# Window attention and a 3x3 convolution in one kernel: in every second window the two heads of a pair change halves of the key axis

## Time and profile before

| | |
|---|---|
| median of 3 runs | 3809.45 us (3807.93 to 3814.52) |
| profiled execution: span from the first to the last instruction | 3811.0 us |
| profiled execution: time of its own beside the span | none is recorded; its span stands 0.04% over the median of the runs |
| busy: TensorE matmul, weight load | 92%, 75% of the span |
| busy: VectorE, ScalarE, GpSimd | 81%, 69%, 61% |
| mean granted TensorE clock | 0.97 of 2.4 GHz |
| DMA | 10.5% of 16 engines, 27 GB/s of HBM traffic |

### The profile page before, as it was taken

How to read it: one execution, slowest core, us unless ns; L and a number is a source line. 1 busy time by engine, 2 the same in 40 slices (tenths; PEclk the granted TensorE clock), 3 DMA queues, 4 the chain that set the end, 5 groups by cost and what they waited for, 6 DMA issues and landing times.

```text
span 3811.0 us, 154831 instructions
## 1 busy us (share of the span) xinstructions
PE 3499.2 (92%) x57227; PEld 2843.6 (75%) x57227; DVE 3074.2 (81%) x7552; ACT 2642.8 (69%) x5857; POOL 2316.9 (61%) x3674
## 2 busy tenths in 40 slices
PE   2999999999999999999999999999999999999997
PEld 1677777777777777777777777777777777777775
DVE  5788877888878888788888788887788887888885
ACT  1877776777766677767777667767767777677773
POOL 4476555666555665556765556655556655566663
PEclk9999999999999999999999999999999999999998
DMA  2011110111101111101111101111011111111001
GB/s 54 19 32 34 32 30 24 31 32 34 32 25 27 34 34 32 32 22 32 32 34 34 27 25 32 34 33 33 22 29 32 34 34 27 27 30 34 17 17 30
DMA packets 213494, 115.45 MB, mean 30 GB/s; under 512 B 8784, under 2 KB 212688, under 8 KB 212688
## 3 DMA queue, kind: packets, MB, share of 16 engines
q1 hardware_dynamic: 212688, 104.72, 10.5%
HBM read 53.31 MB, written 51.38 MB: 27 GB/s over the span
## 4 chain that ended last, share of the span: by engine, by line
POOL 48%; issue 38%; PE 7%; DVE 3%; POOLq 2%; ACT 1%; SPq 0%; DMA 0%; DVEq 0%; ACTq 0%
POOL s_sb L408 21%; POOL plane L436 11%; POOL x_n L448 7%; POOL x_n L425 4%; PE conv_ps L998 2%; PE qkv_ps L879 2%; POOL gn_t L392 1%; POOL gn_t L394 1%; PE attn_ps L917 1%; POOL gn_t L393 1%; POOL gn_y L395 1%; PE probsT_ps L903 1%; PE scores_ps L892 1%; POOLq L388 1%; POOLq L405 1%
## 5 line engine op out<-in xcount | busy, mean ns | idle before, releaser
L408 POOL TENSOR_TENSOR s_sb<-s_sb,s_max 113x392 f32<-113x392 f32 x1024 | 1028.1, 1004 | 1304.8 <-DVE s_max L752 1304.4
L464 ACT ACTIVATE probs<-s_sb 113x392 f32<-113x392 f32 x1024 | 551.7, 539 | 195.6 <-POOL s_sb L408 136.9
L903 PE MATMUL probsT_ps<-ident,probs 113*128 113x113 f32 x4096 | 596.6, 269 | 77.8 <-ACT probsT L470 77.7
L470 ACT COPY probsT<-probsT_ps 128x392 f32<-128x392 f32 x1024 | 490.1, 479 | 189.2 <-PE probsT_ps L903 181.5
L917 PEld LDWEIGHTS attn_ps<-v,probsT 128*49 128x49 f32 x16384 | 472.3, 127 | 199.2 <-issue 142.5
L436 POOL TENSOR_TENSOR plane<-x_n 128x224 f32<-128x224 f32 x896 | 591.9, 681 | 30.3 <-POOL x_n L425 23.3
L752 DVE TENSOR_REDUCE s_max<-s_sb 113x8 f32<-113x392 f32 x1024 | 574.8, 561 | 35.4
L531 ACT COPY v<-qkv_ps 64x256 f32<-64x256 f32 (+2 forms) x1280 | 394.1, 328 | 287.2 <-PE qkv_ps L879 281.0
L917 PE MATMUL attn_ps<-v,probsT 128*49 128x34 f32 x16384 | 575.0, 215 | 14.1 <-DVE o_sb L723 11.6
L747 DVE TENSOR_TENSOR s_sb<-scores_ps,bias 113x392 f32<-113x392 f32 x1024 | 566.2, 553 | 13.2 <-PE scores_ps L892 12.5
L892 PE MATMUL scores_ps<-k,q 32*49 32x98 f32 x16384 | 473.6, 254 | 79.8 <-issue 79.8
(11 more groups left out here) (142 smaller groups left out, 6776.6 us busy)
## 6 DMA issues: line engine op xcount, KB each, us to landing
x_in<-in_x_dram SPq DMA_DIRECT2D x224, 224.0 KB, 2.9
out_dram<-x_out SPq DMA_DIRECT2D x224, 224.0 KB, 2.5
x_b<-in_L_conv_w_dram SPq DMA_DIRECT2D x1, 576.0 KB
x_b<-L_conv_pruning_mask_dram SPq DMA_DIRECT2D x1, 576.0 KB
x_n<-_conv_rel_pos_table_dram SPq DMA_DIRECT2D x14, 10.7 KB
x_n<-in_mask_dram SPq DMA_DIRECT2D x1, 196.0 KB
w_in<-n_L_conv_qkv_weight_dram SPq DMA_DIRECT2D x1, 192.0 KB
ident<-in_ident_dram SPq DMA_DIRECT2D x1, 64.0 KB
```

The costliest lines, as they stand in the source:

```text
L408: nc.gpsimd.tensor_tensor(s, s, top, ALU.subtract).then_inc(sub_ready, 1)
L464: nc.scalar.activation(probs[0:QP, slot % 2, :, :, 0:N], s_sb[0:QP, slot % 4], ACT.Exp)\
L470: nc.scalar.copy(probsT[:, slot % 2], probsT_ps[:].rearrange("p (w n) -> p w n", n=ODD)[:, :, 0:N])\
L903: last = nc.tensor.transpose(probsT_ps[:, w * 128:w * 128 + QP], probs[0:QP, u % 2, w].rearrange("p e m -> p (e m)"), ident[0:QP, 0:QP])
```

## The change

In the odd windows the two heads of a pair change places on the key axis: the even head goes to the upper half of partitions (64 on) and the odd head to the lower. A pair of neighbouring windows then needs the same kind of head in both halves: even heads where the first window is even, odd heads where it is odd. So v's weight columns are sorted in the setup into 64 columns of the even heads and 64 of the odd ones (VC), step 2 takes the four runs that begin with an even window and moves the 64 even columns, and step 3 takes the other runs and moves the 64 odd columns. The number of matmuls and of weight loads stays, 27 a row; the moving operand is half as long. The last run of step 3 gets a place of its own for each of its halves in qkv_ps.

k, v and the bias follow: ScalarE writes the two copies of k into changing places (two ACTIVATEs as before, with a pattern of four windows by two by 49), v is evacuated with two copies in either step, each 64 partitions by 256, the columns of ones are set window parity by window parity (four memsets for two), and the bias is added half by half (16 instructions for 8), with the pair's heads reversed in the upper half. The copy of the turned weights in the setup becomes two.

```diff
--- before.py
+++ after.py
@@ -49,6 +49,7 @@
 QP = ODD + N
 RT = WIN * W
 VW = 2 * HD + 2
+VC = PAIRS * HD
 TAPS = 9
 PLANES, KW = 4, 3
 TILE_ROWS = 8
@@ -518,18 +519,19 @@
                         if j == 0:
                             last = nc.scalar.activation(q[:, slot], tokens, ACT.Identity, bias=q_bias[:], scale=q_scale[:])
                         elif j == 1:
-                            for e in range(2):
-                                last = nc.scalar.activation(k[:, slot, :, e, :], tokens, ACT.Identity,
-                                                            bias=k_bias[:, e:e + 1], scale=k_scale[:, e:e + 1])
+                            by_half = k[:, slot].rearrange("p (a b) x n -> p a (b x) n", b=2)
+                            for e, places in enumerate((slice(0, 4, 3), slice(1, 3))):
+                                last = nc.scalar.activation(by_half[:, :, places, :],
+                                                            qkv_ps[:, 0:RT].rearrange("p (a b n) -> p a b n", b=2, n=N),
+                                                            ACT.Identity, bias=k_bias[:, e:e + 1], scale=k_scale[:, e:e + 1])
                         else:
 
-                            parts = ([(0, 4, 0, 0), (0, 4, 1, 1)] if j == 2 else
-                                     [(0, 4, 4, 0), (0, 3, 5, 1), (3, 1, 0, 1)])
-                            vals = qkv_ps[:].rearrange("p (w a e d) -> p w a e d", w=NWIN // 2, e=2, d=HD)
-                            for b, n, w0, e in parts:
-                                half = slice(ODD * e, ODD * e + ODD)
-                                last = nc.scalar.copy(v[half, slot, w0:w0 + n, :, e * HD:(e + 1) * HD],
-                                                      vals[half, b:b + n, :, e, :])
+                            e = j - 2
+                            vals = qkv_ps[:].rearrange("p (b a d) -> p b a d", a=PAIRS, d=HD)
+                            for half in range(2):
+                                parts, first = slice(ODD * half, ODD * half + ODD), e * (1 - half)
+                                last = nc.scalar.copy(v[parts, slot, (half ^ e)::2, :, e * HD:(e + 1) * HD],
+                                                      vals[parts, first:first + NWIN // 2, :, :])
                         last.then_inc(qkv_free, 1)
                     misc(i, u, END)
                     row = u - HI_AT
@@ -583,7 +585,9 @@
             step(vec.memset(ones, 1.0))
             for e in range(2):
 
-                step(vec.memset(v[ODD * e:ODD * e + N, :, :, :, 2 * HD + e:2 * HD + e + 1], 1.0))
+                for b in range(2):
+                    at = 2 * HD + (e ^ b)
+                    step(vec.memset(v[ODD * e:ODD * e + N, :, b::2, :, at:at + 1], 1.0))
             dve.wait_ge(const_in, 16 * N_CONST)
 
 
@@ -602,7 +606,10 @@
                 step(vec.tensor_scalar(w_f[:, t, :], w_in[:, t, :], w_inv[:, t:t + 1], None, ALU.mult))
             dve.sem_inc(qkv_scaled, 1)
             dve.wait_ge(setup_pe, 2)
-            step(vec.tensor_copy(w_f[:, 0:3, :], misc_ps[:, 0:3 * C].rearrange("p (t c) -> p t c", c=C)))
+            step(vec.tensor_copy(w_f[:, 0:2, :], misc_ps[:, 0:2 * C].rearrange("p (t c) -> p t c", c=C)))
+
+            step(vec.tensor_copy(w_f[:, 2, :].rearrange("p (e a d) -> p e a d", e=2, d=HD),
+                                 misc_ps[:, 2 * C:3 * C].rearrange("p (a e d) -> p e a d", e=2, d=HD)))
 
             step(vec.tensor_copy(w_in[:, 3, :], misc_ps[:, 3 * C:4 * C]))
             step(vec.tensor_scalar(w_f[:, 3, :], w_in[:, 3, :], w_max[:, 2:3], None, ALU.mult))
@@ -656,9 +663,13 @@
             dve.wait_ge(rel_ready, 1)
             for a in range(2):
                 for pair in range(PAIRS):
-                    two = rel[0:QP, 2 * pair:2 * pair + 2, :]
-                    last = vec.tensor_tensor(bias[0:QP, a, pair], two.unsqueeze(1).to_broadcast((QP, WP, 2, N)),
-                                             mask[0:QP, a].unsqueeze(2).to_broadcast((QP, WP, 2, N)), ALU.add)
+                    for half, parts in enumerate((slice(0, ODD), slice(ODD, QP))):
+                        n = parts.stop - parts.start
+                        two = rel[parts, 2 * pair:2 * pair + 2, :]
+                        if half == 1:
+                            two = two[:, ::-1, :]
+                        last = vec.tensor_tensor(bias[parts, a, pair], two.unsqueeze(1).to_broadcast((n, WP, 2, N)),
+                                                 mask[parts, a].unsqueeze(2).to_broadcast((n, WP, 2, N)), ALU.add)
             step(last)
             dve.wait_ge(zeroed, 1)
             for row in (0, H + 1):
@@ -936,14 +947,17 @@
 
 
 
-                    runs = [(b * C, slice(0, 128), (j - 2) * 4 + b) for b in range(4)]
-                    if j == 3:
-                        runs[3:] = [(3 * C, slice(0, ODD), NWIN - 1), (3 * C, slice(ODD, 128), 0)]
-                    for col, parts, w in runs:
+                    if j == 2:
+                        runs = [(b, slice(0, 128), 2 * b) for b in range(4)]
+                    else:
+                        runs = [(b + 1, slice(0, 128), 2 * b + 1) for b in range(3)]
+                        runs += [(4, slice(0, ODD), NWIN - 1), (0, slice(ODD, 128), 0)]
+                    of = slice((j - 2) * VC, (j - 1) * VC)
+                    for b, parts, w in runs:
                         at, width = (row * NWIN + w) * ODD, parts.stop - parts.start
                         hi, lo = (t[:].rearrange("p w n -> p (w n)")[:, at:at + width] for t in (tok_hi, tok_lo))
-                        last = three(qkv_ps[parts, col:col + C],
-                                     ((hi, wT_hi[:, 2, :]), (lo, wT_hi[:, 2, :]), (hi, wT_lo[:, 2, :])))
+                        last = three(qkv_ps[parts, b * VC:(b + 1) * VC],
+                                     ((hi, wT_hi[:, 2, of]), (lo, wT_hi[:, 2, of]), (hi, wT_lo[:, 2, of])))
                 last.then_inc(qkv_ready, 1)
 
             def misc(i, u, kind, t):
```

## The result

The changed kernel takes 3909.86 us (median of 4 runs, 3906.50 to 3912.67), the kernel before 3809.97 us on the same chip: a ratio of 1.0259, interval 1.0246 to 1.0272. The prediction was 3719, range 3670 to 3772, with 0.06 for slower.

The account below looks back on a forecast made before the run. TensorE was taken as nearly full (92% busy), though VectorE and GpSimd hold part of the chain. 2.80 + 0.16 = 2.96 us an image, 94.7 us over 32, less 4.2 setup, gave 90.5 us saved: 3719 us, range 3670 to 3772.

Parts of the forecast that it names:

- The price of a matmul: TensorE, v's matmuls: 64 columns less take each from 57 to 30 ns, 0.63 us a row, 5.0 us an image.
- rival (b): v's short matmuls run no faster, held by loads or issue (also the microcode rule): 3808 to 3813 us, chance 0.08.
- Setup and ScalarE: Setup costs 4.2 us more; ScalarE's v copies, four of 371 ns for five, save 0.16 us an image.
- price of k's pattern: ScalarE's two k evacuations, one more pattern dimension: at most 1.3 us an image, taken as nothing.
- What reaches the end: Per image: 2.52 us from four rows on TensorE's chain plus 0.28 us elsewhere, 2.80; with ScalarE 2.96 us.
- the assignment of rows 0, 3, 6 and 7 to TensorE: v's blocks in these rows lie where the chain is TensorE's, so each row's full 0.63 us counts.
- VectorE's waits before x_b: Expected sign in the profile: VectorE's waits before x_b shrink by about half.
- rival (d): Clock halves twice a loop image, after the plane_lo and probsT waits: 106 us paid, 3825 us, chance 0.06.
- both waits pass in the loop at full clock today: Argument against the twice-slow-clock case: TensorE's plane_lo (0.63 us) and probsT (1.26 us) waits bring no slow clock.
- The wait for plane_lo: TensorE's loop-image wait for VectorE, said to grow from 0.63 to 1.9 us and perhaps trigger slow clock.
- This wait grows [...] to 2.5 us: TensorE's 1.26 us probsT wait grows by what rows 4 and 5 save; slow-clock-once case, 3771 us, chance 0.10.
- two stretches of 3.4 us at 0.55 us for each: Slow-clock price in the twice case: 3.4 us more at half clock costs 1.9 us, twice in each loop image.

Follow-up runs that it names:

- e10: Kernel before with only the loop's branches told ahead (hint_back_edge) on every engine: 3680.84 us, ratio 0.9659.
- e9: Changed kernel with only the loop's branches told ahead, three Newton steps kept: 3656.44 us, ratio 0.9600 to the kernel before.
- e7: Changed kernel with v's matmuls moving 128 columns again, halves of the last run side by side: 3818.15 us, ratio 1.0018 to the kernel before.
- e14: Changed layout with 128 columns in v's matmuls and the loop's branches told ahead: 3688.90 us, ratio 0.9682 to the kernel before.
- e15: Changed kernel, no hint, 12 more matmuls in unit 2 of each image: 3841.31 us, ratio 1.0067 to the kernel before.
- e17: Changed kernel with branches told ahead and 12 more matmuls in unit 2 of the loop's images alone: 3677.46 us, ratio 0.9649 to the kernel before.
- e6: Changed kernel with 20 filler matmuls ahead of each wait, in units 10 and 26: 3856.22 us, ratio 1.0117 to the kernel before.
- e3: Changed kernel with two Newton steps for three in each group norm: 3704.08 us, ratio 0.9721 to the kernel before.
- e5: Kernel before with two Newton steps for three in each group norm: 3706.93 us, ratio 0.9722.
- e8: Changed kernel with 20 filler matmuls in unit 10 alone, ahead of unit 11's wait: 3813.73 us, ratio 1.0010 to the kernel before.
- e16: Kernel before, no hint, 12 more matmuls in unit 2 of each image: 3844.60 us, ratio 1.0085.
- e11: Changed kernel with two Newton steps and the loop's branches told ahead: 3540.60 us, ratio 0.9288 to the kernel before.
- e12: Kernel before with two Newton steps and the loop's branches told ahead: 3583.28 us, ratio 0.9396.
- e13: Changed kernel with branches told ahead and 12 more matmuls in unit 2 of each image: 3870.72 us, ratio 1.0168 to the kernel before.
- e18: Changed kernel with branches told ahead and 24 more matmuls in unit 2 of the loop's images alone: 3822.41 us, ratio 1.0030 to the kernel before.

## Why the prediction was wrong, point by point

**The price of a matmul: right.** 57 to 30 ns, to the nanosecond; rival (b), with its rule of microcode, is out. TensorE's waits took the gain back in part: from e10 to e9, both at full clock, the one in unit 11 grew from 1.21 to 1.50 us, the one for gn_var from 0.53 to 0.85, the one for plane_lo from 0.62 to 0.91.

**Setup and ScalarE: right.** First scores 5.1 us later (4.2 expected), and v's four copies a row are what they were to be:

```profile
L533 ACT COPY v<-qkv_ps 64x256 f32<-64x256 f32 x1024 | 381.9, 373 | 178.9 <-PE qkv_ps L890 169.1
```

The feared price of k's pattern is not there: L524 takes 684 ns on average, and e7's and e14's loop images show next to no loss.

**What reaches the end: mis-sized, 2.96 us an image for 1.1.** Three pairs at full clock give 1.1 to 1.2 (109.3 to 108.2, 110.3 to 109.2, 107.5 to 106.4). By rows of windows, from e10 to e9: -0.62, -0.04, +0.06, -0.33, -0.62, +0.48, +0.10, -0.15 us. The step that failed is the assignment of rows 0, 3, 6 and 7 to TensorE: the whole 0.63 comes through in rows 0 and 4 only, half in row 3, almost none in 6 and 7. Row 4 is one that the chain gave to others; one chain, followed back from one end, doesn't tell what a row would do if TensorE were faster. Row 5 loses: TensorE waits 0.7 to 0.8 us there for VectorE's conv_y, which it did not before. Why VectorE is later was not settled; some of its operations take longer at another time, an example in the last section. That VectorE's waits before x_b would shrink by half was wrong too; in the unrolled image they grew from 7.0 to 8.7 us.

**The clock: the step that decided.** The sum that gave 3719 us puts the change's effect on the clock at nothing. What the runs show in its place is a cost of 4.3 us in each loop image, four times what the change gains there. The clock was in the text as rival (d), at 0.06 and 3825 us, 85 us short of the measurement. Three things in it failed.

- Its case against itself, "that both waits pass in the loop at full clock today", does not fit its own rows: the fourth image, in the earlier trace rows, is the loop's second, and the next two have the same slow stretch behind the same wait. It also rested on a list with a hole. The wait for plane_lo never mattered. The one that did, 1.23 us in unit 11, was not in the earlier trace rows: it is as long as the wait in unit 26, and it is preceded by v's first block, which the change shortens.
- "This wait grows [...] to 2.5 us" was not how it came about. The wait in unit 26, of which this was said, stayed at 1.26 us, and its slow stretches came with the moment. The wait in unit 11 grew, by 0.28 us to 1.51, and that was enough where 1.23 never was. The prediction looked at the size of a wait alone. In e15 and e17 a wait of 1.50 us is followed by either clock.
- The price: two stretches of 3.4 us at 0.55 us for each, 3.8 us an image. There are 13.6 us, at 0.35 for each: 112.9 us with them against 108.2 in e6's image, 4.7 us. The mean over the loop hid what one full-clock image beside a slow one shows.

The account with the sizes as measured, which sorts the loss and does not test it, since the 4.3 us are what is left over: 3810, plus 5 for the setup, less 1.1 us in each of 29 images (32 us), plus 4.3 us for the slow clock in each of the loop's 28 (the 3.2 us that one got longer on average, and the 1.1 by which it should have got shorter; 120 us) and 4.7 us in the image behind the loop: 3908 us.

**Also failed: that a loop image is the sum of its work.** The changed kernel's loop images are mostly 119.5 us, those before 116.0, e3's and e5's 112.5, and e8's and e7's are at 116 once more. e3 and e5 differ by 1.1 us of work an image and by nothing in time; e3 has 51 us more slow clock in its loop (184 against 133). e16 and e17 show that the lengths between also occur.

**What stays open.** The runs show that long waits in units 11 and 26 are needed for the slow stretches inside a loop image (e3, e5, e11, e12), that filling the first removes its stretch (e6, e8), and that the length of a wait and its moment decide together (the waits side by side). They don't show how long a wait at a given moment has to be, nor does any run foretell at which moment the waits of a new version will come. They don't show either why the pause came back in e13 and e18 and a second one came in e6; e13 and e18 have more instructions ahead of or inside the loop than e17, and e6 more than e8.

## What to carry to other kernels

Where the granted clock is under 1.00 in the profile before, a change is worth what it does to the clock first and to the work second: list every wait of TensorE over a microsecond in one whole image with the clock behind it, and expect work taken from in front of such a wait to lengthen the wait. A wait of the same length costs nothing or several us by its moment, so a time of such a kernel holds for its exact length only. Judge a small saving at full clock, as an image without a slow stretch or with the disturbance removed, and test it at a second length of the loop's body: here the same edit is 2.6% slower, equal, 0.7% or 1.2% faster by what stands around it. Look for the trigger on the engines that are not busy: four operations of 128x1 less in each group norm on GpSimd (one Newton step, so a coarser inverse square root) and a hint at the loop's branch took 6.0% off the kernel before (e12) and 9.4% off the changed one (e11).

## What was not expected of the hardware

- **More work, less time.** 12 matmuls more in each image took 69 us from the changed kernel (e15) and gave 33 us to the one before (e16).
- **The clock falls with TensorE far from idle.** Before the stretch at 3654.2 the engine waited 1.51 us and no longer; in the earlier trace rows 1.26 us was enough, and by its moment the same 1.26 us is followed by full clock in 25 of 28 loop images of the kernel before.
- **The pause at a loop's end, about 2.9 us, is the branch's.** With the hint it is gone inside the loop in e9 to e12, e14 and e17, and with it the 6.8 us of slow clock: 110.3 for 116.0 us an image. It comes once, behind the loop, 2.3 to 3.1 us. The Trainium skill ("Runtime: NRT & Kernel Launch", "Instruction fetch mechanics") says that a taken branch to a target outside the fetched pages has to wait for that page to be loaded. The trace agrees: in the last 3 us before the loop image at 2249.2 the kernel before has three packets on its queues for instructions, and e10 has none in the 3.3 us before its image at 1720.3. That the hint's effect is lost when the code is a few instructions longer (e13, e18) is not explained by any run here.
- **The same VectorE operation can take half as long again or more at another time.** The seven of an unrolled image in the changed kernel (minimum, median and maximum in ns):

```profile
L846 DVE SCALAR_TENSOR_TENSOR result<-conv_y,wc_scale,x_c x7: 683/686/1020, 3618.6 to 3717.4; 128x448 f32<-128x448 f32 x7
```

In the same image of the kernel before the longest of the seven is 717 ns, but over the whole run the longest is 1.17 us there and 1.18 us in the changed kernel. What does it was not tried.
